# Early tiles of a routed expert layer taken from fewer blocks, with padded list rows and last-group scatters paced by other engines

## Chip, cores and metric

One core of one Trainium2 chip. The metric is the device time of one execution in microseconds (us), as the median of repeated runs; lower is better.

## What is computed

Two residual branches on x of shape (16, 128, 256), float32 throughout. The first is a long convolution over the products of eight context channels with each other, per head, contracted with the layer norm of x. The second, which the change touches, is a mixture of 32 experts (hidden 256, expert width 176) with six experts per token, chosen within four of eight groups, and a shared expert of double width:

```python
logits = xf @ w_router                       # xf: layer norm of x, 2048 tokens
scores = sigmoid(logits); sfc = scores + corr_bias
# four of eight groups by the sum of their two best, then the best six experts of these
combine[t, topk_idx] = scores[t, topk_idx]
eo = einsum('etm,emh->eth', silu(g) * u, down_w)        # g, u: xf by gate_w, up_w
routed = einsum('te,eth->th', combine, eo)
shared = silu(xf @ sh_gate_w) * (xf @ sh_up_w) @ sh_down_w
x = x + tanh(g_ffn) * (routed + shared)
```

## The kernel before

The 2048 tokens are 16 blocks of 128 (`B` = 16), handled in `NG` = 4 groups of `GB` = 4 blocks. The work has two parts.

**Groups.** `group(g, attend, route)` is written out on TensorE (PE), ScalarE (ACT) and VectorE. A call routes group g and does the attention of group g + 1; the last one, group 3, only routes. Routing a group means: normalize its rows into `payload` (even groups) or `payload_2` (odd groups), transpose them, logits (L1118), scores (L520), choice of six experts per token (`choose`), ranks of the tokens in their experts' lists by small matmuls (L1140 to L1147), slots (`place_rows`, L765), and the shared expert block by block (`shared_up`, `shared_hT`, `shared_down`, with `silu`, `copy_sh_hT` on ACT and `shared_times`, `add_shared` on VectorE). GpSimd (POOL) then scatters each block's rows, with token number and scores behind the 256 values, into the experts' lists in DRAM (`expert_lists`, L395): 24 scatters per group of 128 rows each, at most `AHEAD` = 6 in flight. When all of a group have landed it increments `payload_free` (L400), which so counts 1 before group 0 and g + 2 after group g.

**Tiles.** Afterwards each tile takes 128 rows of one expert's list: SP loads it (`load_tile`, L313) into one of `NX` = 4 slots of `payload`, PE transposes it (`xT`, L1196), VectorE copies it (L973), PE multiplies by gate and up weights (L1207), ACT and VectorE make silu(g) * u (L554, L991), PE transposes (L1217) and multiplies by the down weights (L1226), ACT scales by the token's score (L569), and POOL adds the rows into `token_sums` (L410). VectorE's `pick` reads score and token number from the loaded rows. Results wait in a ring of `YR` = 16 rows of buffers. SP loads a tile once tile t - 4 is transposed and picked.

The tile table is made on the chip. To start early, `NA` = 16 tiles come from full tiles among the lists of the groups known first: after group 2, i.e. from `KNOWN` = 12 blocks, with PE's counting matmuls at L1149 to L1154 and `describe_known` (from L827) and `spread_known` on VectorE, over the first `EA` = `WD_MID` = 18 experts. The rest is described by `describe_tiles` after the last group's ranks, `spread_tables` signals `tables_ready`.

**Weights.** All experts' weights end up in SBUF in one `arena`, on top of the buffers of the first part, so they can be loaded only as these come free. Gate and up weights of experts 0 to 13 (`EARLY` = 14) are loaded early. After the last attention, SP loads down weights of experts 0 to 17 and gate and up weights of 14 to 17 (L323, L324); ACT loads gate and up weights of 18 to 31 after the last group's scores (L524) and the remaining down weights in two DMAs (L545, L548) before its tile loop. PE waits for SP's loads before tile 0 (L1253, L1254) and for ACT's three before tile 16 (`last_in`, L1202).

SP's order around the change: down and up weights (L322 to L324), wait for the early table (L325), wait for `payload_free` of group 2 (L326), tiles 0 to 15, then wait for the whole table and for group 3's scatters (L333), tiles 16 on. POOL's order: scatters of groups 0 to 3, then the adds.

Of the kernel before, what the change touches and what calls it, by code (L numbers as in the profile page):

```python
# [9 lines left out]
GB = 4  # L10
# [17 lines left out]
ROW = L + 1 + E  # L28
TOK_AT, SCORE_AT = L, L + 1
# [30 lines left out]
assert ROUTER_AT + KC * E <= ARENA  # L60
# [3 lines left out]
WD_LAST = (X2T_AT - WD_AT) // WD_E // 2 * 2  # L64
assert WD_AT <= TMP_AT
# [13 lines left out]
assert TE_AT + NTILES <= WORK and NX <= GB  # L79

# [6 lines left out]
KNOWN = (NG - 1) * GB  # L87
EA = WD_MID
# [3 lines left out]
def build(nc, x, ctx_t, toeplitz, g_xattn, g_ffn, skip_d, w_router, corr_bias,  # L92
# [10 lines left out]
    with ctx:  # L103
# [18 lines left out]
        y_rows = sb("y_rows", [P, 3, L])  # L122
# [115 lines left out]
        y_at = [(y_rows, i * L) for i in range(3)] + [(blank, 0)]  # L238
        y_at += [(b, i * L) for b in (q_sb, shgu_sb, shd_sb) for i in range(4)]
        y_row = lambda t: win(*y_at[t % YR], [[1, L]])  # L240
        pick_w = lambda t: win(work, TW_AT + t % NPICK, [[1, 1]])
# [31 lines left out]
        def _(sp):  # L273
# [34 lines left out]
            def load_tile(t):  # L308
# [4 lines left out]
                sp.dma_start(payload[:, t % NX, :], lists[bass.ds(first, P), :]).then_inc(t_loaded[t % NX], 16)  # L313
# [9 lines left out]
            load_down(sp, 0, WD_MID, late_in)  # L323
            load_up(sp, EARLY, WD_MID, late_in)  # L324
            sp.wait_ge(tables_a_ready, 1)  # L325
            sp.wait_ge(payload_free, NG)  # L326
            for t in range(NX):
                load_tile(t)
            for t in range(NX, NA):
                load_tile(t)  # L330
# [21 lines left out]
        def _(pool):  # L352
# [25 lines left out]
            link(nc.gpsimd.tensor_scalar(tok_id[:, :], win(lane_dump, 0, [[0, B]]), float(B), None, ALU.mult))  # L378
            link(nc.gpsimd.tensor_tensor(tok_id[:, :], tok_id[:, :], iota_e[:, 0:B], ALU.add))
# [7 lines left out]
            for g in range(NG):  # L387
                pool.wait_ge(slots_ready, g + 1)
                pool.sem_inc(held, 1)
                for b in range(GB):  # L390
                    for k in range(TOPK):
                        sent = (g * GB + b) * TOPK + k
                        if sent >= AHEAD:
                            pool.wait_ge(scattered[sent % AHEAD], sent // AHEAD * 16)
                        nc.gpsimd.indirect_dma_start(  # L395
# [35 lines left out]
        def _(act):  # L431
# [18 lines left out]
            def group(g, attend, route):  # L450
# [51 lines left out]
                if route:  # L502
# [17 lines left out]
                    nc.scalar.activation(pay[g % 2][:, :, SCORE_AT:ROW], win(bank[4], 0, [[E, GB], [1, E]]),  # L520
                                         ACT.Sigmoid).then_inc(scores_ready, 1)
# [775 lines left out]
```

## Time and profile before

| | us |
|---|---|
| median of 3 runs (544.68 to 546.29) | 544.88 |
| profiled execution, its own time | 550.49 |
| profiled execution, span of the program | 548.6 |
| PE busy, TensorE's mean granted clock 0.903 | 445.5 (81%) |
| VectorE busy | 312.8 (57%) |
| POOL busy | 288.6 (53%) |
| ACT busy | 203.9 (37%) |
| DMA moved 85.38 MB | mean 156 GB/s |

Busy time counts instructions, not waits; matmuls are pipelined and their ends are modelled, so a busy PE isn't PE at its peak. Times within the execution are counted from the span's start. DMA share is the mean busy share of the core's 16 DMA engines. PEclk is the granted part of TensorE's full clock.

### The profile page before, as it was taken

How to read it: one execution, taken by the hardware profiler on the slowest of the kernel's cores; microseconds unless marked ns; L12 is line 12 of the kernel's file. 1: busy time of each engine (PE TensorE's matmuls, PEld its weight loads, DVE VectorE, ACT ScalarE, POOL GpSimd, SP SyncE). 2: the span in 40 equal slices, each digit the busy share in tenths (PEclk: the TensorE clock that was granted, in tenths of full speed). 3: DMA queues.
4: the chain of work that ended last, by engine and by line, in shares of the span. 5: the costliest groups of instructions: out<-in, count | busy, mean ns of one | idle time of the engine just before them, and what ended most of it. 6: DMA issues, size and time to landing. Idle time of an engine off the chain costs nothing.

```text
span 548.6 us, 8656 instructions
## 1 busy us (share of the span) xinstructions
PE 445.5 (81%) x2114; PEld 334.4 (61%) x2114; DVE 312.8 (57%) x1163; ACT 203.9 (37%) x522; POOL 288.6 (53%) x224
## 2 busy tenths in 40 slices
PE   0924989798888668646999999999999999999900
PEld 0724767666766456424777777777777777777700
DVE  3999999859968755303444444444444444444307
ACT  3531725533462322002444444444444444444400
POOL 2000038848884752771556566665656566656630
PEclk9985989989988959755999999999999999999965
DMA  7999302222221499983666666566656665666569
GB/s 260 357 302 404 156 32 84 97 87 101 90 98 55 146 257 340 357 292 106 108 116 107 118 110 121 108 118 106 121 108 118 107 121 106 119 108 122 67 145 351
DMA packets 56053, 85.38 MB, mean 156 GB/s; under 512 B 6492, under 2 KB 47676, under 8 KB 55740
## 3 DMA queue, kind: packets, MB, share of 16 engines
q1 hardware_dynamic: 33566, 46.68, 28.8%
q0 software_dynamic: 20160, 28.37, 26.7%
q10 hardware_dynamic: 2270, 9.68, 4.6%
q8 instruction: 23, 0.38, 0.3%
q14 instruction: 34, 0.28, 0.2%
HBM read 44.91 MB, written 39.80 MB: 154 GB/s over the span
## 4 chain that ended last, share of the span: by engine, by line
PE 61%; DVE 22%; issue 7%; DMA 4%; ACT 2%; another core or an unknown queue 2%; SPq 1%; POOL 1%; DVEq 0%; POOLq 0%; ACTq 0%
PE bank L1207 24%; PE bank L1226 17%; DVE arena L658 5%; PE bank L1196 5%; PE bank L1217 4%; PE bank L1069 3%; DVE arena L636 3%; PE bank L1090 3%; DVE arena L666 3%; DMA arena<-token_sums 2%; DVE arena L615 1%; DMA rows<-x 1%; PE bank L1079 1%; PE bank L1040 1%
## 5 line engine op out<-in xcount | busy, mean ns | idle before, releaser
L395 POOL DMA_INDIRECT expert_lists<-payload,slots x96 | 116.7, 1216 | 126.3 <-DVE slots L765 84.3
L1207 PE MATMUL bank<-wgu,work 128*128 x432 | 149.8, 470 | 6.8 <-issue 5.2
L1226 PE MATMUL bank<-wd,work 88*128 x432 | 111.9, 382 | 0.0
L991 DVE TENSOR_TENSOR work<-work,bank 128x176 f32<-128x176 f32 x108 | 36.4, 337 | 128.2 <-ACT work L554 113.6
L1207 PEld LDWEIGHTS bank<-wgu,work 128*128 128x128 f32 x432 | 75.2, 194 | 31.8 <-issue 9.5
L554 ACT ACTIVATE work<-bank 128x176 f32<-128x176 f32 x108 | 34.2, 317 | 125.5 <-PE bank L1207 96.9
L1226 PEld LDWEIGHTS bank<-wd,work 88*128 88x128 f32 x432 | 73.9, 191 | 6.2 <-issue 0.2
L973 DVE COPY work<-bank 128x256 f32<-128x256 f32 x108 | 45.8, 424 | 34.4 <-PE bank L1196 18.6
L410 POOL DMA_INDIRECT token_sums<-q_sb,dest x28 | 43.6, 1558 | 27.2 <-ACT q_sb L569 7.3
L410 POOL DMA_INDIRECT token_sums<-shgu_sb,dest x28 | 43.6, 1559 | 24.8 <-DMA token_sums<-shgu_sb,dest 6.8
L1217 PEld LDWEIGHTS bank<-ident,work 128*88 128x88 f32 x216 | 26.5, 123 | 37.7 <-issue 18.8
L410 POOL DMA_INDIRECT token_sums<-shd_sb,dest x24 | 37.4, 1558 | 22.2 <-DVE work L985 7.7
L410 POOL DMA_INDIRECT token_sums<-y_rows,dest x21 | 32.8, 1561 | 29.7 <-ACT y_rows L569 15.3
L1217 PE MATMUL bank<-ident,work 128*88 128x128 f32 x216 | 41.8, 275 | 6.6 <-DVE work L991 6.6
L1040 PE MATMUL bank<-arena 128*128 128x288 f32 x128 | 45.8, 442 | 1.5 <-DVE arena L643 1.0
L1069 PE MATMUL bank<-shgu_sb,arena 128*128 128x352 f32 x128 | 46.5, 512 | 0.0
L658 DVE TENSOR_TENSOR arena<-arena,q_sb 128x448 f32<-128x448 f32 (+7 forms) x120 | 45.4, 454 | 0.0
L1196 PE MATMUL bank<-ident,payload 128*128 128x128 f32 x216 | 42.8, 280 | 0.7 <-issue 0.7
L561 ACT COPY work<-bank 88x256 f32<-88x256 f32 x108 | 39.7, 367 | 0.1
L1196 PEld LDWEIGHTS bank<-ident,payload 128*128 128x128 f32 x216 | 31.3, 146 | 12.6 <-issue 2.1
L457 ACT COPY arena<-bank 128x288 f32<-128x288 f32 x64 | 25.3, 399 | 26.7 <-PE bank L1041 23.4
L1069 PEld LDWEIGHTS bank<-shgu_sb,arena 128*128 128x128 f32 x128 | 26.2, 216 | 12.5 <-issue 4.0
(170 smaller groups left out, 570.1 us busy)
## 6 DMA issues: line engine op xcount, KB each, us to landing
payload<-expert_lists SPq DMA_DIRECT2D x108, 144.5 KB
wgu<-w_gu SPq DMA_DIRECT2D x1, 4928.0 KB, 19.1
wgu<-w_gu ACTq DMA_DIRECT2D x1, 4928.0 KB
expert_lists<-blank SPq DMA_DIRECT2D x1, 4768.5 KB, 25.4
arena<-token_sums SPq DMA_DIRECT2D x8, 512.0 KB, 7.3
wd<-w_down SPq DMA_DIRECT2D x1, 3168.0 KB
token_sums<-blank SPq DMA_DIRECT2D x1, 2304.0 KB, 28.9
arena<-toeplitz ACTq DMA_DIRECT2D x2, 1024.0 KB, 10.5
```

The source lines that it names most:

```text
L395: nc.gpsimd.indirect_dma_start(lists, bass.IndirectOffsetOnAxis(ap=slots[:, g % 2, b, k:k + 1], axis=0), pay[g % 2][:, b, :], None).then_i ...
L410: nc.gpsimd.indirect_dma_start(sums, bass.IndirectOffsetOnAxis(ap=dest[:, t % NPICK:t % NPICK + 1], axis=0), y_row(t), None, compute_op=AL ...
L561: nc.scalar.copy(win(work, HT_AT + t % 2 * L, [[1, L]], parts=MH), bank[4 + t % 2][0:MH, 0:L]).then_inc(t_hT_copied, 1)
L658: last = nc.vector.tensor_tensor(win(arena, Z_AT + z0, [[DH * DH, CELLS], [1, DH - d]]), y, win(q_sb, q_at + i0, [[DH, CELLS], [1, DH - d] ...
L973: nc.vector.tensor_copy(win(work, XT_AT + t % 2 * L, [[1, L]]), bank[t % 2][:, 0:L]).then_inc(t_x, 1)
L991: nc.vector.tensor_tensor(win(work, H_AT + t % 2 * M, [[1, M]]), win(work, SG_AT + t % 2 * M, [[1, M]]), bank[2 + t % 2][:, M:2 * M], ALU. ...
L1040: nc.tensor.matmul(y[:, 0:2 * CB], toe(h, 0), prods(s, hh, 0, 2), start=True, stop=False)
L1069: last = nc.tensor.matmul(bank[5 + half][:, 0:SHM], x2T(b, k), shgu_sb[:, k, half * SHM:(half + 1) * SHM], start=(k == 0), stop=(k == KC - 1))
L1196: last = nc.tensor.transpose(bank[t % 2][:, k * P:(k + 1) * P], payload[:, t % NX, k * P:(k + 1) * P], ident[:, :])
L1207: last = nc.tensor.matmul(bank[2 + t % 2][:, 0:2 * M], xT_half(t, k), wgu[:, bass.ds(e * WGU_E + k * 2 * M, 2 * M)], start=(k == 0), stop= ...
L1217: last = nc.tensor.transpose(bank[4 + t % 2][0:MH, c * P:(c + 1) * P], win(work, H_AT + t % 2 * M + c * MH, [[1, MH]]), ident[:, :])
L1226: last = nc.tensor.matmul(bank[6 + t % 2][:, 0:L], hT_half(t, c), wd[:, bass.ds(e * WD_E + c * L, L)], start=(c == 0), stop=(c == 1))
```

## The change

Rows of the lists get 304 elements (1216 bytes) instead of 289 (1156); the added 15 are zeroed once. The early table is made after group 1, from 8 blocks and over 14 experts. Tiles 0 to 7 are loaded into four slots at the end of the arena instead of `payload`, once group 1's scatters have landed; tiles 8 to 15 go to `payload`, once group 2's have. SP loads only the down weights of experts 0 to 13; all others go in pairs of experts from ACT, six DMAs in the last group, the others one or two per tile in tiles 0 to 8. POOL's scatters of the last group, but the first, wait for VectorE's steps of the shared expert (`sh_h_ready`) and, from the 13th, for PE's tile transposes (`t_xT`). The ring of 16 result rows is laid out over other buffers, as `y_rows` has one less.

```diff
-ROW = L + 1 + E
-TOK_AT, SCORE_AT = L, L + 1
+ROW = -(-(L + 1 + E) // 16) * 16
+TOK_AT, SCORE_AT, SCORE_END = L, L + 1, L + 1 + E
...
+TILES_AT = ROUTER_AT + KC * E
+assert TILES_AT + 4 * ROW <= ARENA
...
+WD_TILES = (ROUTER_AT - WD_AT) // WD_E // 2 * 2
+LATE = [n for n in range(EARLY, E, 2)]
...
+IN_ARENA = 2 * NX
...
-KNOWN = (NG - 1) * GB
-EA = WD_MID
+KNOWN = (NG - 2) * GB
+EA = EARLY
...
+        tile_rows = lambda t, at, n: (win(arena, TILES_AT + t % NX * ROW + at, [[1, n]]) if t < IN_ARENA
+                                      else payload[:, t % NX, at:at + n])
...
             sp.wait_ge(pairs_summed, 2 * NG)
-            load_down(sp, 0, WD_MID, late_in)
-            load_up(sp, EARLY, WD_MID, late_in)
+            load_down(sp, 0, EARLY, late_in)
+            sp.wait_ge(payload_free, NG - 1)
             sp.wait_ge(tables_a_ready, 1)
+            for t in range(IN_ARENA):
+                load_tile(t)
             sp.wait_ge(payload_free, NG)
-            for t in range(NX):
-                load_tile(t)
-            for t in range(NX, NA):
+            for t in range(IN_ARENA, NA):
                 load_tile(t)
...
+            for p in pay:
+                nc.gpsimd.memset(p[:, :, SCORE_END:ROW], 0.0)
...
+                        nth_of = b * TOPK + k
+                        if g == NG - 1 and 0 < nth_of < GB * TOPK // 2:
+                            pool.wait_ge(sh_h_ready, g * GB + 1 + nth_of // 3)
+                        elif g == NG - 1 and nth_of:
+                            pool.wait_ge(t_xT, 1 + (nth_of - GB * TOPK // 2) // 2)
...
+                    if not attend:
+                        act.wait_ge(pairs_summed, 2 * NG)
+                        load_up(act, EARLY, EARLY + 2, last_in)
...
                     silu(0)
                     if not attend:
-                        load_up(act, WD_MID, E, last_in)
+                        load_up(act, EARLY + 2, EARLY + 4, last_in)
...
+                        if not attend:
+                            load_up(act, EARLY + 4 + 2 * b, EARLY + 6 + 2 * b, last_in)
...
+            def late_weights(t):
+
+                if t < 3:
+                    n = EARLY + 12 + 2 * t
+                    load_up(act, n, n + 2, last_in)
+                if t < len(LATE):
+                    n = LATE[t]
+                    if n == WD_LAST:
+                        act.wait_ge(sh_stored, 16 * (B - GB))
+                        act.wait_ge(sh_added, GB)
+                    if n == WD_TILES:
+                        act.wait_ge(t_xT, IN_ARENA)
+                        act.wait_ge(t_picked, IN_ARENA)
+                    load_down(act, n, n + 2, last_in)
+
             act.wait_ge(tables_ready, 1)
-            load_down(act, WD_MID, WD_LAST, last_in)
-            act.wait_ge(sh_stored, 16 * (B - GB))
-            act.wait_ge(sh_added, GB)
-            load_down(act, WD_LAST, E, last_in)
...
                     copy_y(t - 2)
+                if t < NA:
+                    late_weights(t)
...
-                    if g == NG - 2:
+                    if g == NG - 3:
                         nc.vector.tensor_copy(count_a[:, :], bank[4][:, 2 * GB * E:(2 * GB + 1) * E])
...
-                    pe.wait_ge(last_in, 48)
+                    pe.wait_ge(last_in, 2 * len(LATE) * 16)
...
-            pe.wait_ge(late_in, 32)
+            pe.wait_ge(late_in, 16)
```

## Rows read from the trace of the kernel before

**Rows 1.** Busy time by stretch; columns as in the first line.

```profile
core 0: us, PE busy (x) PEld busy (x) DVE busy (x) ACT busy (x) POOL busy (x), PEclk, DMA share, GB/s
...
100.00:150.00 50.00, 42.45 (x206) 33.17 (x204) 41.50 (x132) 21.46 (x47) 36.57 (x27) 0.93 0.25 90
190.00:200.00 10.00, 5.44 (x25) 4.64 (x24) 3.17 (x20) 4.25 (x8) 4.84 (x6) 0.50 0.94 254
...
207.00:226.00 19.00, 16.46 (x103) 12.63 (x103) 11.53 (x53) 3.13 (x6) 6.99 (x8) 1.00 1.02 374
...
230.00:240.00 10.00, 4.72 (x12) 2.22 (x10) 1.29 (x5) 0.00 (x0) 7.56 (x9) 0.50 0.82 301
...
230.47:257.19 26.72, 12.68 (x30) 6.81 (x28) 4.61 (x20) 1.57 (x5) 13.44 (x14) 0.50 0.66 230
...
250.00:260.00 10.00, 8.43 (x26) 5.75 (x27) 3.36 (x17) 2.31 (x7) 1.25 (x1) 0.61 0.23 65
...
300.00:400.00 100.00, 100.00 (x485) 74.07 (x483) 46.04 (x202) 42.69 (x121) 62.67 (x41) 1.00 0.65 114
```

**Rows 2.** Chain of waits late in the tile loop: start us, us, what.

```profile
509.44 1.19 PE bank L1207 x4
...
511.93 1.19 PE bank L1207 x4
```

**Rows 3.** Page, DMA queue of ACT (packets, MB, share) and DMA issues.

```profile
q10 hardware_dynamic: 2270, 9.68, 4.6%
...
payload<-expert_lists SPq DMA_DIRECT2D x108, 144.5 KB
...
wgu<-w_gu ACTq DMA_DIRECT2D x1, 4928.0 KB
expert_lists<-blank SPq DMA_DIRECT2D x1, 4768.5 KB, 25.4
```

**Rows 4.** Chain of waits from 190 to 260 us.

```profile
193.96 5.06 another core or an unknown queue
...
230.47 0.43 PE bank L1196 x2
...
240.49 9.01 issue
...
250.55 1.41 PE bank L1196 x2
...
257.40 0.43 PE bank L1196 x2
```

**Rows 5.** Timeline: start us, us, instruction, [idle before <- releaser]; scatters, loads, early table.

```profile
163.52 0.96 POOL L395 DMA_INDIRECT expert_lists<-payload,slots  x1 [0.30 <-issue]
...
188.38 0.32 SPq L260 DMA_DIRECT2D wd<-w_down  x1
...
205.95 0.39 ACTq L255 DMA_DIRECT2D wgu<-w_gu  x1
...
207.16 0.07 DVE L877 MEMSET tile_dump<- 128x16 f32 x1
...
217.84 43.18 SPq L313 DMA_DIRECT2D payload<-expert_lists  x9
...
217.96 0.96 POOL L395 DMA_INDIRECT expert_lists<-payload,slots  x1 [10.19 <-issue]
...
247.04 0.96 POOL L395 DMA_INDIRECT expert_lists<-payload,slots  x1 [0.30 <-issue]
```

**Rows 6.** Timeline: the early table's steps on VectorE, first steps of the tile loop.

```profile
188.44 0.38 DVE L847 TENSOR_TENSOR arena<-count_a,tile_at 128x216 f32<-128x216 f32 x1
...
198.16 0.19 DVE L860 TENSOR_TENSOR taken_a<-arena 128x32 f32<-128x32 f32 x1 [1.82 <-remote]
...
199.65 0.29 DVE L868 COPY arena<-arena 128x256 f32<-128x256 f32 x1
...
235.11 0.42 DVE L973 COPY work<-bank 128x256 f32<-128x256 f32 x1 [3.08 <-issue]
...
249.15 0.32 ACT L554 ACTIVATE work<-bank 128x176 f32<-128x176 f32 x1 [22.32 <-issue]
```

More of the change, by code:

```diff
@@ L59 @@
 ROUTER_AT = SHOUT_AT + 2 * L
-assert ROUTER_AT + KC * E <= ARENA
+TILES_AT = ROUTER_AT + KC * E
+assert TILES_AT + 4 * ROW <= ARENA
 STATS_AT, MOMENTS_AT, NEWTON_AT = TMP_AT, TMP_AT + 6 * B, TMP_AT + 8 * B
@@ L121, in build @@
         payload_2 = sb("payload_2", [P, GB, ROW])
-        y_rows = sb("y_rows", [P, 3, L])
+        y_rows = sb("y_rows", [P, 2, L])
         blank = sb("blank", [P, ROW])
@@ L237, in build @@
         hT_half = lambda t, c: win(work, HT_AT + t % 2 * L + c * P, [[1, P]], parts=MH)
-        y_at = [(y_rows, i * L) for i in range(3)] + [(blank, 0)]
-        y_at += [(b, i * L) for b in (q_sb, shgu_sb, shd_sb) for i in range(4)]
+        y_at = [(y_rows, i * L) for i in range(2)] + [(blank, 0)]
+        y_at += [(b, i * L) for b, n in ((q_sb, 4), (shgu_sb, 5), (shd_sb, 4)) for i in range(n)]
         y_row = lambda t: win(*y_at[t % YR], [[1, L]])
+        tile_rows = lambda t, at, n: (win(arena, TILES_AT + t % NX * ROW + at, [[1, n]]) if t < IN_ARENA
+                                      else payload[:, t % NX, at:at + n])
         pick_w = lambda t: win(work, TW_AT + t % NPICK, [[1, 1]])
@@ L312, in load_tile @@
                 first = table_value(sp, tile_row, t, E * LIST)
-                sp.dma_start(payload[:, t % NX, :], lists[bass.ds(first, P), :]).then_inc(t_loaded[t % NX], 16)
+                sp.dma_start(tile_rows(t, 0, ROW), lists[bass.ds(first, P), :]).then_inc(t_loaded[t % NX], 16)
             def load_block(n):
@@ L519, in group @@
                     act.wait_ge(logits_ready, g + 1)
-                    nc.scalar.activation(pay[g % 2][:, :, SCORE_AT:ROW], win(bank[4], 0, [[E, GB], [1, E]]),
+                    nc.scalar.activation(pay[g % 2][:, :, SCORE_AT:SCORE_END], win(bank[4], 0, [[E, GB], [1, E]]),
                                          ACT.Sigmoid).then_inc(scores_ready, 1)
@@ L708, in flat @@
                         return win(arena, o, [[step, n]])
-                    scores = pay[g % 2][:, :, SCORE_AT:ROW]
+                    scores = pay[g % 2][:, :, SCORE_AT:SCORE_END]
                     sfc = tmp(GB, E)
@@ L977, in pick @@
                 mask = win(work, MASK_AT + t % 2 * E, [[1, E]])
-                nc.vector.scalar_tensor_tensor(mask, iota_e[:, :], tile_e[:, t:t + 1], payload[:, t % NX, SCORE_AT:ROW],
+                nc.vector.scalar_tensor_tensor(mask, iota_e[:, :], tile_e[:, t:t + 1], tile_rows(t, SCORE_AT, E),
                                                ALU.is_equal, ALU.mult).then_inc(t_masked, 1)
@@ L981, in pick @@
                     dve.wait_ge(t_added[t % NX], nth(t - NPICK))
-                nc.vector.tensor_scalar(dest[:, t % NPICK:t % NPICK + 1], payload[:, t % NX, TOK_AT:TOK_AT + 1],
+                nc.vector.tensor_scalar(dest[:, t % NPICK:t % NPICK + 1], tile_rows(t, TOK_AT, 1),
                                         tile_dump[:, t:t + 1], float(t % S * SUM_ROWS), ALU.max, ALU.add)
@@ L1148, in group @@
                                             start=False, stop=True)
-                    if g == NG - 2:
+                    if g == NG - 3:
                         for seen in range(KNOWN):
@@ L1196, in xT @@
                     last = nc.tensor.transpose(bank[t % 2][:, k * P:(k + 1) * P],
-                                               payload[:, t % NX, k * P:(k + 1) * P], ident[:, :])
+                                               tile_rows(t, k * P, P), ident[:, :])
                 last.then_inc(t_xT, 1)
```

## The prediction

> **What bounds the kernel now.** I read the windows first. From 300 to 400 us TensorE is busy all the time at the full clock (2.4 GHz) with DMA at 0.65 [rows 1]; the matmuls of two tiles in a row start 2.49 us apart [rows 2], and the 108 tiles [rows 3] take half of the span. Nothing in the diff touches that stretch. The stretch between the shared experts and the running tile loop is different: from 230.47 to 257.19 us PE shows 12.68 us of work in 26.72, all at the low clock (1.2 GHz), with DMA at 0.66 and, from 230 to 240, at 0.82 [rows 1]. The chain puts the first tile's transposes at 230.47 and those of the fifth at 257.40, 26.9 us for four tiles that cost 4 x 2.49 = 10.0 us in the steady loop: **17.0 us are lost here**. The chain's largest piece is 9.01 us of "issue" at 240.49; tile 3 is reached at 250.55, so a tile took (250.55 - 230.47)/3 = 6.7 us [rows 4].
>
> Why is it slow? The queues [rows 5] show what flies. Group 1's last scatter leaves at 163.52. A pair of experts has 704 KB of gate and up weights (4928/7 [rows 3]) and, by the shapes, 352 KB of down weights. At 188.38 SP puts nine pairs down and behind them two pairs up on its queue, 4.6 MB; at 205.95 ACT adds seven pairs up, 4.9 MB. POOL waits 10.19 us for group 2's scatters to land, until 217.96, and only then does SP start the tile loads (217.84), although the table that they need is done at 207.16. The last group's 24 scatters go out back to back from 217.96 to 247.04. The engine rows [rows 6] show the second symptom, which I weigh most: signals come late. PE's transposes of tile 0 stand at 230.47, the copy that waits for them at 235.11; ACT's first silu stands at 249.15 after 22.32 us idle, for which the profile finds no releaser. The same is seen earlier: from 190 to 200 (DMA 0.94) ScalarE waits 5.06 us for logits and a VectorE step waits 1.82 us for VectorE's own signal [rows 4, 6]. But from 207 to 226, with DMA at 1.02, PE is busy 16.46 of 19 us at the full clock [rows 1]. So a full DMA alone doesn't make signals late; late stretches are those in which POOL's scatters run on and on beside weight loads. That is read from three stretches of one trace, not proved.
>
> **The change, part by part.**
> Early tiles from groups 0 and 1 and 14 experts: the tables come from 1024 tokens. The reference, run on the drawn inputs, sends 794, 836 and 722 of them to experts 0, 1 and 11: 6 + 6 + 5 full tiles, at least 16. So the 16 early tiles are all real, 91 remain, and the loop still runs 108. Cost of tiles: 0. The counting matmuls move from group 2 to group 1 and shrink from 12 to 8; the comparison at L847 (0.38 us [rows 6]) shrinks from 216 to 112 columns. Both under 0.3 us; 0.
>
> First eight tiles in the arena: their loads wait for group 1's scatters (over soon after 163.52) and the table, so they start at about 207.2 instead of 217.84 [rows 5]. Only four are in flight at a time, but these have 22 us until PE is free; before, they had 12 under the heaviest load. This covers the first wait.
>
> Weights in pairs from ACT: SP's load at 188 shrinks from 4.6 MB to 2.5 MB (down weights of 14 experts), ACT adds one pair (0.7 MB) before the logits. That lightens 188 to 200, where the planner's chain runs from 188.44 to 199.65 + 0.29 [rows 6], 11.5 us, and the shared experts cannot start before it. What can come back: at least 0, at most about the 5.06 us wait [rows 4]. I take 3.0, a little above the middle, as 2.1 of 4.6 MB go and 0.7 come. ACT issues 18 loads instead of three. One costs 0.39 us [rows 5]; two per tile in the first three tiles make 1.07 (42.69 us per 100 us, at 2.49 per tile [rows 1]) + 0.78 = 1.85 us of the 2.49: hidden. If the cover goes, it is 0.8 us for three tiles. Past 229 us there remain three pairs up and nine pairs down, 5.4 MB; ACT's queue moved 9.68 MB in 4.6% of 548.6 us, 25.2 us [rows 3], so they need 14.1 us of all engines. They are due at tile 16, 40 us later, and PE's one wait for all 18 stands there.
>
> The Trainium skill ("DMA: Bandwidth & Descriptors", section Bandwidth) speaks against the pairs: it wants at least 1 MiB per DMA for 75% of the peak, and these are 0.7 and 0.35 MB. At its 341 GB/s for 1 MB, as an estimate by that page, the 5.4 MB would take 15.9 us and not 14.1. By it the sum is the same, and the busy stretch ends some 2 us later, which makes the slower rival more likely.
>
> Scatters of the last group: each of the first 12 waits for a third of a shared block, each later pair for one more transposed tile. What is queued behind on POOL: the other scatters, and then all adds into token_sums. Who waits: SP's loads from tile 16 on, and ACT's ring of 16 result rows. The 24th scatter goes out with tile 5's transposes, some 13 us into the loop; landing took at most 10.19 [rows 5]; the first add so starts near tile 9, under the 16 rows of the ring, and POOL, busy 62.67 us in 100 [rows 1], catches up. Price: 0; if the first add slips 15 us further, PE waits for it.
>
> Rows of 1216 bytes: 5.2% more bytes in blanks, scatters and tile loads. The blanks landed in 25.4 us [rows 3], so 1.3 us later, long before the first scatter, under VectorE's work. In the loop DMA goes from 0.65 to at most 0.68: hidden. Whether aligned rows move faster no row shows: between 0 and the 5.2% they cost; I take 0. Two small memsets on POOL at the start: hidden by SP's earlier loads.
>
> **The sum**, in the profiled execution. Lost now: 17.0. After the change still lost: the first hand-overs, half of 235.11 - 230.47 [rows 4, 6] = 2.3, rounded to 2.5 with the load of the tile's number; the low clock at the start, as between 250 and 260, where a mean of 0.61 means 7.8 us at half clock [rows 1], so 3.9 us; and remaining lateness, between 0 and the 10.6 that are left of 17.0: I take a quarter, 2.6, as half of the scatters and a third of the bytes are gone by then. That is 9.0. Gain 17.0 - 9.0 + 3.0 = 11.0. The profiled execution took 550.49 us for a span of 548.6, 1% over the median of 544.88. 550.49 - 11.0 = 539.5, times 544.88/550.49 gives **534.0**. Within this case: 529 (no lateness, all of 5.06) to 540 (6 us of lateness, nothing at the front).
>
> **Rivals.**
> Everything prompt and the clock never falls: PE passes from the shared experts to tiles without a pause. Gain 17.0 - 2.5 + 3.0 = 17.5, 527.5. For: tiles are there. Against: before, PE's clock was low already at the first tile [rows 1], after the wait for VectorE's tables, and that wait stays. 0.13.
>
> Contention only moves. Tiles still take 6.7 us until the traffic ends. The work after 229: 14.1 us of weights, 12 scatters at 0.25 x 50/27 = 0.46 us each (100 to 150 us, 27 POOL instructions [rows 1]), 5.6 us, and eight tile loads at a third of 0.65 x 2.49 = 1.6 us per tile, 4 us: until 229 + 24 = 253. By then 3.6 tiles are done; before, the steady line stood at 4 - (257.4 - 253)/2.49 = 2.2. Gain 1.4 x 2.49 = 3.4: 541.5. For: the same bytes, fewer moved before 229. 0.20.
>
> **Slower.** The same rate, but it feeds itself: weights and scatters are now released by the tiles' own steps. At 6.7 us per tile the last scatter leaves at 229 + 5 x 6.7 = 262, the last weights later still, and the catching-up adds join. If the crawl ends at 265, 5.4 tiles are done where before had 4 + 7.6/2.49 = 7.1: 4.2 us lost, 549.0. It decides at 258.4, where both lines meet. For: all late rows lie where scatters and weights fly together, and the new order brings both into the loop. Against: slower release also thins the traffic. 0.15.
>
> The change doesn't reach the wait: tile loads were not what PE waited for, and lateness has another cause that stays. Then 544.9. For: the longest pieces carry no tile load as releaser. 0.05.
>
> The forecast has the remaining 0.47. A measurement of this kernel tells 0.3%, 1.6 us, from no change; faster by more: 0.47 + 0.13 + 0.20 less 0.04 of the moved contention = 0.76; within: 0.05 + 0.04 = 0.09; slower: 0.15. The range goes from 524.5, one below the best rival with all of the front's 5.06 (gain 19.6, 525.5), to 546.5, which leaves out most of the slower case.
>
> **What would show it.** Tile loads starting at about 207 and group 2's scatters landed before 210. The planner's chain under 9 us. From the first tile's transposes to the fifth's 14 to 20 us instead of 26.9. L554's idle time without one wait of 22 us. Last weights landed before tile 16. Still 108 tiles at 2.49 us. The forecast is wrong if a tile takes over 5 us in the first eight, if the gap at 230 remains with little DMA about (then lateness isn't contention), or if PE waits at tile 16 or for the ring.

## The result, and the profile after

The changed kernel took **552.46 us** (median of four runs, 550.64 to 557.7) beside 545.59 us for the kernel before: ratio **1.0111** [1.0058, 1.0164], slower by about 1.1%. The forecast was 534.0 us. The ratio is estimated from the single runs in the faster of the chip's two states and so is not the quotient of the two medians. The profiled execution of the changed kernel took 551.01 us for a span of 549.0. That of before had taken 550.49 us for 548.6, above its own median, so the two profiles are equally long while the medians are 1.1% apart. The profiles show how the work moved; for a difference of one per cent I go by the ratios of runs on one chip.

The page of the changed kernel, its span, queues, chain and DMA issues. ACT's late weights, before three loads of which one had 4928 KB [rows 3], are now eighteen small ones, and the blanks are 5% larger by the longer rows (4768.5 KB before), though they landed in 23.3 us and not 25.4 [rows 3]:

```profile
span 549.0 us, 8688 instructions
...
PEclk9985989899989668789999999999999999999755
DMA  7999212222223686598666666666667665675559
...
q10 hardware_dynamic: 2907, 11.84, 6.4%
...
PE 62%; DVE 18%; DMA 7%; issue 5%; ACT 3%; another core or an unknown queue 3%; POOL 1%; SPq 1%; DVEq 0%; POOLq 0%; ACTq 0%
...
wgu<-w_gu ACTq DMA_DIRECT2D x9, 704.0 KB
expert_lists<-blank SPq DMA_DIRECT2D x1, 5016.0 KB, 23.3
...
wd<-w_down ACTq DMA_DIRECT2D x9, 352.0 KB
```

Busy time by stretch, the changed kernel (columns as in the first line). These answer to [rows 1]:

```profile
core 0: us, PE busy (x) PEld busy (x) DVE busy (x) ACT busy (x) POOL busy (x), PEclk, DMA share, GB/s
...
230.00:240.00 10.00, 8.74 (x29) 5.57 (x28) 3.73 (x16) 0.90 (x3) 6.36 (x7) 0.63 0.64 208
240.00:250.00 10.00, 6.52 (x31) 4.47 (x30) 3.14 (x15) 3.06 (x9) 5.16 (x6) 1.00 1.02 342
250.00:260.00 10.00, 9.43 (x45) 6.45 (x44) 3.77 (x17) 3.66 (x11) 2.96 (x2) 1.00 0.81 273
300.00:400.00 100.00, 100.00 (x484) 74.08 (x483) 46.28 (x203) 42.57 (x121) 62.30 (x40) 1.00 0.66 117
```

From 230 to 260 TensorE does 24.7 us of work, where before it did 16.0, and from 240 on it is at the full clock (2.4 GHz), where before it was at the low one until 250 and for most of the time to 260. The gap at which the forecast aimed has mostly closed: the transposes of the first tile start at 230.40 and those of the fifth at 240.42, 10.0 us in place of 26.9. What is left of it comes after. The chain of waits has the third tile's transposes, a tile load and the ninth tile's transposes (start us, us, what):

```profile
235.43 0.43 PE bank L1227 x2
...
246.70 8.59 DMA payload<-expert_lists
...
255.34 0.44 PE bank L1227 x2
```

Six tiles took 19.9 us where the steady loop takes 14.9, and the ninth tile, the first that is loaded into `payload`, waited 8.59 us for its load, beside late weights and scatters (DMA at 1.02). The steady loop is unchanged. Yet the end did not move. The chain also shows what ends last in the changed kernel (start us, us, what; L598 writes the result row, L423 adds it into `token_sums`, L348 starts the reading of the sums):

```profile
507.34 0.88 PE bank L1257 x4
508.22 0.02 issue
508.24 0.48 ACT shgu_sb L598
508.72 0.60 issue
509.33 3.67 DMA token_sums<-q_sb,dest
...
513.85 1.46 POOL token_sums L423
...
520.72 3.70 DMA token_sums<-shgu_sb,dest
...
525.27 3.76 DMA token_sums<-shgu_sb,dest
...
529.22 0.34 SPq L348
...
532.82 10.27 DMA arena<-token_sums
```

PE's last matmul ends near 509.1; before it ended at 521.0. **TensorE is 11.9 us earlier** in this pair of profiles, and for 20 us nothing but adds runs: one every 2.3 us. An add holds POOL for 1.56 us and has landed about 3.7 us after its start, and the add after next waits for that landing, because the sums are kept in two copies (S = 2). The last add starts at 525.27; before, at 525.38. How the delay arose is in the timeline of POOL, changed kernel (start us, us, instruction, [idle before <- releaser]):

```profile
247.77 0.96 POOL L408 DMA_INDIRECT expert_lists<-payload,slots  x1 [0.30 <-issue]
256.74 1.61 POOL L423 DMA_INDIRECT token_sums<-y_rows,dest  x1 [8.01 <-issue]
258.66 1.58 POOL L423 DMA_INDIRECT token_sums<-y_rows,dest  x1 [0.30 <-issue]
265.59 1.56 POOL L423 DMA_INDIRECT token_sums<-blank,dest  x1 [5.35 <-DVE work L1016]
267.94 1.56 POOL L423 DMA_INDIRECT token_sums<-q_sb,dest  x1 [0.80 <-issue]
...
300.21 1.56 POOL L423 DMA_INDIRECT token_sums<-y_rows,dest  x1 [0.40 <-issue]
```

And the same of before:

```profile
258.75 1.61 POOL L410 DMA_INDIRECT token_sums<-y_rows,dest  x1 [10.75 <-ACT y_rows L569]
261.50 1.58 POOL L410 DMA_INDIRECT token_sums<-y_rows,dest  x1 [1.14 <-ACT y_rows L569]
263.98 1.56 POOL L410 DMA_INDIRECT token_sums<-y_rows,dest  x1 [0.89 <-ACT y_rows L569]
```

Before, the adds wait for result rows (the first was ready at 257.9). In the changed kernel the first row is ready at 243.9, but POOL still has scatters until 247.77 and then waits 8.01 us for them to land. The third add waits again, 5.35 us, for the landing of the first: the profile names a step of VectorE (L1016, the pick), but the pick of this add's own tile had ended at 239.0, and in a repeat, below, the profile names the landing itself. The seventeenth add, that of the first tile behind the 16 early ones, starts at 300.21, against 299.5 before. From there to the last add it is 225.1 us for 91 adds, 2.47 us each, while PE makes a tile in 2.49. From there on the adds run 13 to 16 us behind the results to the end, where before it was mostly 1 to 3 us: before, the adds kept up with the rows, now they wait for each other.

**Theory A**: the chain of adds sets the end. The changed kernel ends some 249 us after its seventeenth add starts, whatever PE does. The letters of the rivals are those of the recorded expectations. **B**: the loss is a disturbance that only unprofiled runs had. **C**: POOL's own pace or the DMA limits the adds, and not the wait for a landing. **D**: the pacing of the scatters is what helped PE, and without it PE is late again. **E**: the longer rows cost time. **F**: the late weights in small loads, beside the first adds, slow these down. Two more have no letter: PE's gain is lost elsewhere and the adds only follow, and POOL's wait for the landing of the scatters ahead of the first add is what delays the adds.

### The profile page after: what moved, and what is told of

Its sections match the earlier page's. It is cut to its first block, busy times and chain, and to the rows that moved or that the text cites. A ratio compares the mean times of both kernels' runs of the same rounds, so it can differ in the third digit from the quotient of the medians.

```text
span 549.0 us, 8688 instructions
## 1 busy us (share of the span) xinstructions
PE 442.6 (81%) x2110; PEld 333.2 (61%) x2110; DVE 312.2 (57%) x1163; ACT 203.8 (37%) x522; POOL 286.8 (52%) x226
## 3 DMA queue, kind: packets, MB, share of 16 engines
q10 hardware_dynamic: 2907, 11.84, 6.4%
## 4 chain that ended last, share of the span: by engine, by line
PE 62%; DVE 18%; DMA 7%; issue 5%; ACT 3%; another core or an unknown queue 3%; POOL 1%; SPq 1%; DVEq 0%; POOLq 0%; ACTq 0%
PE bank L1238 23%; PE bank L1257 16%; PE bank L1121 4%; PE bank L1100 4%; PE bank L1227 4%; PE bank L1248 4%; DVE arena L689 4%; DVE arena L667 2%; PE bank L1071 2%; DVE arena L697 2%; DMA arena<-token_sums 2%; PE bank L1110 2%; DMA payload<-expert_lists 2%; PE bank L1091 1%
## 5 line engine op out<-in xcount | busy, mean ns | idle before, releaser
L408 POOL DMA_INDIRECT expert_lists<-payload,slots x96 | 114.7, 1195 | 128.9 <-DVE slots L796 88.9
L1238 PE MATMUL bank<-wgu,work 128*128 x432 | 147.8, 465 | 1.3 <-DVE work L1004 1.3
L423 POOL DMA_INDIRECT token_sums<-shgu_sb,dest x35 | 54.5, 1558 | 34.4 <-ACT shd_sb L598 10.8
L423 POOL DMA_INDIRECT token_sums<-q_sb,dest x28 | 43.6, 1558 | 24.6 <-DMA token_sums<-q_sb,dest 8.5
L423 POOL DMA_INDIRECT token_sums<-shd_sb,dest x24 | 37.4, 1557 | 21.0 <-DVE work L1016 6.4
L1227 PE MATMUL bank<-ident,payload 128*128 128x128 f32 x200 | 38.5, 273 | 0.2 <-DMA payload<-expert_lists 0.2
L470 ACT COPY arena<-bank 128x288 f32<-128x288 f32 x64 | 25.4, 399 | 25.9 <-PE bank L1072 22.3
L1227 PEld LDWEIGHTS bank<-ident,payload 128*128 128x128 f32 x200 | 28.3, 142 | 10.9 <-DMA payload<-expert_lists 1.0
L1121 PE MATMUL bank<-shd_sb,arena 88*128 88x256 f32 x128 | 32.2, 396 | 1.9 <-issue 0.7
## 6 DMA issues: line engine op xcount, KB each, us to landing
expert_lists<-blank SPq DMA_DIRECT2D x1, 5016.0 KB, 23.3
```

The costliest lines, as they stand in the source:

```text
L408: nc.gpsimd.indirect_dma_start(lists, bass.IndirectOffsetOnAxis(ap=slots[:, g % 2, b, k:k + 1], axis=0), pay[g % 2][:, b, :], None).then_i ...
L423: nc.gpsimd.indirect_dma_start(sums, bass.IndirectOffsetOnAxis(ap=dest[:, t % NPICK:t % NPICK + 1], axis=0), y_row(t), None, compute_op=AL ...
L1121: last = nc.tensor.matmul(bank[4][:, 0:L], win(arena, HST_AT + c * P, [[1, P]], parts=MH), shd_sb[0:MH, c, :], start=(c == 0), stop=(c == 3))
L1227: last = nc.tensor.transpose(bank[t % 2][:, k * P:(k + 1) * P], tile_rows(t, k * P, P), ident[:, :])
L1238: last = nc.tensor.matmul(bank[2 + t % 2][:, 0:2 * M], xT_half(t, k), wgu[:, bass.ds(e * WGU_E + k * 2 * M, 2 * M)], start=(k == 0), stop= ...
```

## Experiments

Ratios are to the kernel before on the same chip, with their 95% interval. Chips differ (the kernel before had medians from 537.22 to 551.05 us on them), so profiles are compared within one chip where a few us decide.

**The changed kernel again.** No edit.

> The changed kernel once more, as the base of the others on the same chip. Theory A (the chain of adds sets the end): each add into token_sums waits for the landing of the one two before it, which makes about 2.48 us per add, as much as PE needs per tile; PE ends near 508 us, the last add goes out near 525, and the profiled span stays near 549. Theory B (the loss is a disturbance that only unprofiled runs had): the ratio to before comes out near 1.00 here. A alone gives a ratio of 0.995 to 1.005; the first result was 1.011, and a ratio above 1.006 says that something more than A costs time.

Measured: 1.0107 [1.0051, 1.0163], 554.79 us beside 549.82. The seventeenth add started at 301.4, and PE ended at 510.6 of a span of 551.9. The slowdown is real and of the size first seen, and B falls. The expectation had set 0.995 to 1.005 for A alone and read anything above 1.006 as a second cause. So A explains why PE's gain doesn't reach the end, and not yet why the kernel got slower; the second cause is F, measured further down.

**Three copies of the sums.** An add waits for the third before it; reading takes a copy more.

```diff
-S = 2
+S = 3
...
+                nc.vector.tensor_tensor(a, a, d, ALU.add).then_inc(f_added, 1)
+                dve.wait_ge(f_added, 2 * c + 2)
```

> The changed kernel with three copies of token_sums (S = 3), so that an add waits for the one three before it. Theory A: adds go at 1.9 us until they have caught up with PE, the last add goes out within 3 us of PE's end (near 511), 14 us earlier than with two copies; the third copy adds 2 MB to be read at the end and one more addition per part, 5 to 8 us. Sum 6 to 9 us faster than the changed kernel, about 0.985 to 0.99 of it. Theory C (POOL's own pace or DMA throughput limits the adds, not the wait): adds stay at 2.4 us or more, and the kernel gets 5 to 8 us slower.

Measured: 0.9973 [0.9942, 1.0004]; changed kernel on that chip 1.0107, so 0.987 of it, as expected under A. The timeline of POOL with three copies, near the end:

```profile
509.89 1.56 POOL L423 DMA_INDIRECT token_sums<-shgu_sb,dest  x1 [0.94 <-ACT shgu_sb L598]
512.15 1.56 POOL L423 DMA_INDIRECT token_sums<-shgu_sb,dest  x1 [0.70 <-issue]
514.02 1.56 POOL L423 DMA_INDIRECT token_sums<-shgu_sb,dest  x1 [0.30 <-issue]
515.88 1.56 POOL L423 DMA_INDIRECT token_sums<-shgu_sb,dest  x1 [0.30 <-issue]
```

The last add starts 12.3 us earlier than in the repeat of the changed kernel (528.2), and the seventeenth came 1.3 us after its row. But reading three copies takes 25.5 us from its start at 520.0 to the end, where two take 19.8, and PE ends 2.3 us later. Where the adds are behind, they start 1.86 us apart (the last three lines), with the same 1.56 us on POOL: it is the wait for a landing that made 2.47, and C falls. So the adds were the bound, and the third copy gives part back at the end.

**No pacing.** The waits ahead of the last group's scatters go.

```diff
-                        nth_of = b * TOPK + k
-                        if g == NG - 1 and 0 < nth_of < GB * TOPK // 2:
-                            pool.wait_ge(sh_h_ready, g * GB + 1 + nth_of // 3)
-                        elif g == NG - 1 and nth_of:
-                            pool.wait_ge(t_xT, 1 + (nth_of - GB * TOPK // 2) // 2)
```

> The changed kernel without the waits of the last group's scatters on sh_h_ready and t_xT. Theory A: the first add starts as much earlier as the last scatter lands earlier. Without the waits 24 scatters from 209.5 at 1.26 us end at 240, against 244 to 248 with them, so the adds start at 244 to 250 instead of 256.7, and the end comes 5 to 10 us earlier, if signals are not late. Theory D (the pacing keeps signals prompt): PE's first four tiles go back to 6.7 us each and PE ends near 518; then the adds end no earlier than with the waits, within 2 us.

Measured: 1.0277 [1.0209, 1.0345], far slower. If nothing but the last scatter held the adds back, this had to be faster, since it leaves at 241.58. But the first add starts at 265.84 and the last at 542.31. The windows without pacing (columns as before):

```profile
230.00:240.00 10.00, 0.00 (x0) 0.00 (x0) 0.00 (x0) 0.00 (x0) 7.63 (x8) 0.50 0.53 190
240.00:250.00 10.00, 1.08 (x4) 0.62 (x4) 1.82 (x6) 0.58 (x1) 1.93 (x3) 0.50 0.13 47
```

and its timeline (PE's transposes of the tables, and VectorE's step that reads them):

```profile
224.76 0.83 PE L1199 MATMUL bank<-ident,arena 128*128 128x128 f32 x6
246.38 0.29 DVE L974 CAST tile_row<-bank 128x128 int32<-128x128 f32 x1 [22.30 <-remote]
```

For ten microseconds PE, VectorE and ScalarE do nothing while POOL scatters. PE's transposes of the tables are done at 225.6, but the step of VectorE that reads them starts at 246.38, after 22.30 us idle; PE then waits for VectorE, and ScalarE for PE. Everything goes on 4 us after the last scatter. DMA is at 0.53, and of weights only one load of 704 KB flies there. The first gate-and-up matmul starts at 255.9 (changed kernel: 232.7). D holds, and more strongly than it was put: PE ends at 531.4, expected near 518, and the last add starts 14 us later than in the repeat of the changed kernel, expected within 2 us.

**Plain writes instead of adds.**

```diff
-                    y_row(t), None, compute_op=ALU.add)
+                    y_row(t), None)
```

> The changed kernel with the rows written plainly into token_sums instead of added to it (the accumulation is left out, all waits stay). Theory A: a write without reading lands sooner (the list scatters move the same kind of rows), so the chain of two in flight runs at 2.0 us or less, catches up with PE, and the last one goes out near 511: 12 to 15 us faster. Theory C (POOL's pace is the limit, 1.56 us busy and what lies between): the adds stay at 2.4 us and nothing changes by more than 2 us.

This kernel leaves the accumulation out, so it is for the time alone. Measured: 0.9826 [0.975, 0.9902]. POOL needs 0.96 us in place of 1.56. The writes gain on the results: the seventeenth (297.2) is still 6.2 us behind its row, from the thirtieth on they are 0.8 us behind, and the last starts at 517.3, though the first started at 261.0, later than in the changed kernel. With a quicker chain a front that is no better gives a faster kernel. If PE's gain were lost elsewhere and the adds only followed, neither this nor the third copy could bring it back.

**Before, with the pacing alone.** The five lines above added to the kernel before.

> The kernel before with only the pacing of the last group's scatters added. Theory D (an unbroken run of POOL scatters holds back other engines' signals; pacing is what speeds the start of the tiles): the wait of ScalarE's first silu (22.3 us before) falls under 12 us, PE ends 5 to 12 us earlier than 521, near 511 to 516. With theory A on top, the adds still follow at 2.48 us from a start near 256 to 260, so the total stays within 1% of before. If D is wrong and the lateness comes from the bulk weight loads, PE ends at 520 or later and the first tiles still take over 6 us each.

Measured: 0.9999 [0.9965, 1.0033]. PE ends at 509.5, a little sooner than expected and near the changed kernel's 509.1 and 510.6 in its repeat; ScalarE's longest wait for the first silu is 9.8 us, expected under 12. The last scatter leaves at 250.8, the first add starts at 255.4, the seventeenth at 296.0, the last at 522.8. So the pacing alone makes all of PE's gain, and the time stays as it was: the adds run 9 to 11 us behind the results, where before it was 1 to 3. PE's gain buys nothing while the seventeenth add starts no earlier (295.4 on the same chip without pacing, next run).

**Before, with rows of 1216 bytes alone.**

```diff
-ROW = L + 1 + E
+ROW = -(-(L + 1 + E) // 16) * 16
...
```

> The kernel before with rows of 1216 bytes (and the ring laid out as after). Theory A has nothing for it: list scatters and tile loads carry 5% more, the adds 1024 bytes as before, so a ratio of 0.997 to 1.003. Rival E (padded rows cost in the loaded stretch, where scatters land late): 2 to 5 us slower, ratio 1.004 to 1.01, with group 2's scatters landed after 218.

Measured: 0.9968 [0.9933, 1.0003]. No loss, and E falls; a gain of 0.3% is neither shown nor excluded. This profile (546.34 us) is also the best stand-in for the kernel before at its usual time: first add at 253.2, seventeenth at 295.4, 2.1 us behind its row, PE's end at 516.2, span 544.5. Beside it the adds of the changed kernel on the same chip start 6 us later (301.4), and PE's gain is 5.6 us and not 11.9.

**The early table from three groups.** The changed kernel, with the first tile loads again behind group 2's scatters.

```diff
-KNOWN = (NG - 2) * GB
+KNOWN = (NG - 1) * GB
...
-            sp.wait_ge(payload_free, NG - 1)
+            sp.wait_ge(payload_free, NG)
...
```

> The changed kernel with the early table made from three groups again and the first tile loads behind group 2's scatters. They start then near 209 instead of 205, still 20 us before PE needs them: no difference, within 0.3% of the changed kernel (ratio to before about 1.01). If the earlier table matters, PE's first tile moves and the kernel gets 2 us or more slower than the changed one.

Measured: 1.0091 [1.005, 1.0131], as the changed kernel. Tile loads start at 211.6 in place of 205.7; the seventeenth add at 302.1; PE ends at 510.9. So making the early table a group sooner, the headline of the change, does nothing to the time.

**Late weights spread out.** One late load per tile.

```diff
-                if t < len(LATE):
-                    n = LATE[t]
+                elif t < 3 + len(LATE):
+                    n = LATE[t - 3]
```

> The changed kernel with one late weight DMA per tile (12 tiles) instead of two in each of the first three. Theory A with its start: from 240 to 250 DMA is at 1.02, the last scatter (247.8) lands only at 256.7 and the first two adds at 265; with the weights spread the adds' third starts at 262 to 264 instead of 265.6 and the end comes 1.5 to 4 us earlier than the changed kernel. If the weights don't delay them, no change; if tile 16 then waits for weights, PE's end moves but the adds' does not.

Measured: 1.0117 [1.0055, 1.0179], a miss: 1.5 to 4 us less were expected. Weights now go out until 266.3 (260.6 in the changed kernel), so they lie beside the adds for longer, and the seventeenth starts at 303.8.

**Late weights in bulk.** One load of 6336 KB of gate and up weights in the shared stage, and three of down weights, two of them ahead of the tile loop.

```diff
-                if t < 3:
-                    n = EARLY + 12 + 2 * t
-                    load_up(act, n, n + 2, last_in)
...
+                if t == 7:
...
+                    load_down(act, WD_TILES, E, last_in)
...
+            load_down(act, EARLY, WD_LAST, last_in)
```

> The changed kernel with the weights in bulk again (gate and up of 14 to 31 after the last scores, down in three DMAs). In all seven kernels with two copies so far the span is the start of the 17th add plus 249 to 251 us, so only that start counts. Theory F (late weights beside the first adds slow these down: the third add comes 9 us after the first, and not 5 as in the paced kernel before): with the weights landed before 250 the 17th add starts at 296 to 298 instead of 300 to 304, span 545 to 548, ratio 0.995 to 1.003. If F is wrong, it stays at 300 or later and the ratio at 1.01.

Measured, on a faster chip (before 537.22 us): 0.9971 [0.9944, 0.9999], as F had it. The seventeenth add starts at 285.5 of a span of 534.9; the expectation of 296 to 298 was for a slower chip. The changed kernel itself was not run on this one, so it is repeated side by side below.

**Adds first.** POOL's wait for the landing of the last scatters moves behind the first four adds, in the changed kernel.

```diff
             for t in range(4 * (SURE + 1)):
+                if t == 4:
+                    for landed in scattered:
+                        pool.wait_ge(landed, NG * (GB * TOPK // AHEAD * 16))
+                    pool.sem_inc(payload_free, 1)
                 add_tile(t)
```

> The changed kernel with POOL's wait for the last scatters' landing moved behind the first four adds. Theory A: the first add starts right after the last scatter's issue, near 249, instead of 256.7, unless the results are later; the 17th add comes 4 to 8 us earlier and the kernel gets 4 to 8 us faster than the changed one, ratio 0.996 to 1.003. If the pace of adds under the late weights is the limit and not their start, the gain is under 2 us.

Measured: 0.9964 [0.9929, 0.9999], as expected; seventeenth add at 284.7, span 533.9.

**Before, with pacing and adds first.**

> The kernel before, paced (as x5), with the first four adds ahead of the landing wait. Theory A: the adds start near 251 instead of 255.4, the 17th at 290 to 293 (x5: 296.0); with PE's end near 509.5 the last add goes out near 517. Span 540 to 543, ratio 0.985 to 0.993. If the adds of the first tiles run at 2.5 us whatever their start, and the start is bound by the results, no gain over x5.

Measured: 0.9913 [0.9885, 0.9941], as expected; seventeenth add at 281.4, end of the span at 529.6.

**Bulk weights and adds first together**, in the changed kernel.

> x9 and x10 together: the changed kernel with bulk weights and the first four adds ahead of the landing wait. Theory A with F: both gains add, 17th add at 290 to 294, span 539 to 543, ratio 0.983 to 0.993. Without F it equals x10.

Measured: **0.9899** [0.9855, 0.9943], 531.15 us beside 537.22, the best of all. Its timeline of POOL:

```profile
234.87 0.96 POOL L408 DMA_INDIRECT expert_lists<-payload,slots  x1 [0.30 <-issue]
236.14 1.62 POOL L424 DMA_INDIRECT token_sums<-y_rows,dest  x1 [0.30 <-issue]
238.06 1.58 POOL L424 DMA_INDIRECT token_sums<-y_rows,dest  x1 [0.30 <-issue]
241.10 1.56 POOL L424 DMA_INDIRECT token_sums<-blank,dest  x1 [1.46 <-DMA token_sums<-y_rows,dest]
```

The 8.01 us ahead of the first add are 0.30, the 5.35 ahead of the third 1.46 (on this faster chip). The seventeenth add starts at 279.7, and the span ends at 528.2, 248.5 us later.

**Small and bulk weights on one chip.** The changed kernel and the one with bulk weights, side by side.

> The changed kernel beside x14. Theory F: 17th add at 299 or later counted on a chip where before takes 549, ratio to before 1.006 to 1.014, and at least 1% above x14. If the two agree within 0.5%, F falls and the difference seen so far was the chip.

> x9 again beside x13. Theory F: ratio to before 0.994 to 1.000, its 17th add 3 us or more ahead of that of x13, in the profile of the same chip. If F is wrong, it is as slow as x13.

Measured: 1.007 [1.0037, 1.0103] and 0.9985 [0.9955, 1.0016]. The windows with small loads:

```profile
240.00:250.00 10.00, 7.97 (x36) 5.01 (x36) 3.60 (x18) 3.03 (x9) 5.90 (x7) 1.00 1.02 331
250.00:260.00 10.00, 7.88 (x39) 5.48 (x38) 3.43 (x15) 2.93 (x10) 1.93 (x3) 1.00 0.82 282
```

with bulk loads:

```profile
240.00:250.00 10.00, 6.55 (x22) 3.85 (x21) 2.29 (x10) 2.12 (x7) 5.06 (x6) 0.84 0.72 256
250.00:260.00 10.00, 10.00 (x50) 7.43 (x49) 4.58 (x20) 4.21 (x12) 5.15 (x4) 0.99 0.47 100
```

and POOL's timeline, small loads first:

```profile
257.88 1.61 POOL L423 DMA_INDIRECT token_sums<-y_rows,dest  x1 [7.76 <-ACT q_sb L598]
259.80 1.58 POOL L423 DMA_INDIRECT token_sums<-y_rows,dest  x1 [0.31 <-issue]
266.63 1.56 POOL L423 DMA_INDIRECT token_sums<-blank,dest  x1 [5.25 <-DMA token_sums<-y_rows,dest]
```

then bulk:

```profile
253.94 1.61 POOL L423 DMA_INDIRECT token_sums<-y_rows,dest  x1 [3.44 <-DVE work L1007]
255.86 1.58 POOL L423 DMA_INDIRECT token_sums<-y_rows,dest  x1 [0.30 <-issue]
258.54 1.56 POOL L423 DMA_INDIRECT token_sums<-blank,dest  x1 [1.10 <-DMA token_sums<-y_rows,dest]
```

While the first adds fly, DMA is at 0.82 with small loads and 0.47 with bulk. POOL's wait ahead of the first add is 7.76 against 3.44 us, ahead of the third 5.25 against 1.10. The seventeenth add starts at 302.3 against 296.3, the ends are 551.7 and 547.0. F holds in kind; the difference of 0.85% is a little under the "at least 1%" that it had. With bulk weights the changed kernel is as fast as the one before (0.9985), which is what A alone gives. So the late weights as small loads are the second cause: they make the slowdown.

**Two scatters in flight.** No pacing, but a scatter of the last group waits until the second before it has landed.

```diff
+                        if g == NG - 1 and b * TOPK + k >= 2:
+                            pool.wait_ge(scattered[(sent - 2) % AHEAD], ((sent - 2) // AHEAD + 1) * 16)
```

> The changed kernel without pacing, the last group's scatters limited to two in flight instead of six. If signals are late because of scatters piled up in the DMA queues, no wait of VectorE or ScalarE on PE over 10 us is left between 205 and 262 (x3: 22.3), and PE's first gate-up matmul starts within 4 us of that of x13 (x3: 23 us later than the changed kernel). If it is POOL's unbroken run as such that delays them, it is at least 10 us later than in x13.

Measured: 1.032 [1.0256, 1.0385]. The waits from 205 to 285 (engine, line, what it waited for: us in total, times, longest):

```profile
POOL expert_lists L405 <- DMA expert_lists<-payload,slots: 34.0, 14, 4.1
ACT work L580 <- PE bank L1235: 22.1, 11, 8.5
```

The 22 us standstill is gone: the first gate-and-up matmul starts at 233.0 (233.9 in the changed kernel on that chip), PE ends at 516.1. So the scatters as such don't make the standstill; in these runs it comes only with one unbroken run of them. Whether it is the number in flight, POOL's run without a pause or the rate is not separated, as all three change here. But the scatters run until 275.1, so the adds start at 279.6, the seventeenth at 319.9, and the end comes 247.9 us after it, at 567.8. A's sum holds at this far end too.

**Three copies on the best.** S = 3 in the kernel with bulk weights and adds first.

> x12 with three copies of token_sums. Theory A: x12's last add goes out 11 us behind PE's end; with three copies it follows within 3 us, 8 us earlier, and the third copy costs 6 us at the end (x2: 25.5 us from the start of reading to the end against 19.8). Net 0 to 4 us faster than x12, ratio to before 0.983 to 0.990.

Measured: 0.9923 [0.9889, 0.9957], on another chip than the 0.9899 with two copies, and a miss: 0.983 to 0.990 was expected. The last add does follow PE's end within 3.0 us (515.0), but the longer reading takes that back. A third copy brings nothing to be seen here.

**The theories.** Start of the seventeenth add and end of the span, in the kernels with two copies that add: before 299.5 and 548.6; changed 300.2, 549.0; pacing alone 296.0, 545.8; 1216 bytes 295.4, 544.5; three groups 302.1, 551.2; spread 303.8, 554.8; no pacing 315.4, 565.6; two in flight 319.9, 567.8; best 279.7, 528.2. The difference lies between 247.9 and 251.0 in all of them and in the six others of this kind, while the end of PE's work lies from 28 to 52 us ahead of the end. Where the adds follow the rows at once, as in the kernel before, PE's 2.49 us per tile would give the same distance; where they are behind, the constant is the adds' own. That this chain then is the bound is shown by the third copy and by the plain writes, which shorten it and bring the end forward.

## Why the prediction was wrong

**The gap in front of the tiles: right in kind, lucky in the number.** PE's loss was put at 17.0 us with 9.0 left after the change, so 8.0 gained, and 3.0 more at the front. In the pair of profiles PE's work ended 11.9 us earlier, which is near the 11.0 of the sum only because two errors cancel: 5.1 us were left and not 9.0, and the front gave nothing. From the first tile's transposes to the fifth's it took 10.0 us, better than the forecast's 14 to 20; the low clock ended at 240 instead of beyond 250. The cause was named only in part: "late stretches are those in which POOL's scatters run on and on beside weight loads", but hardly any weight loads are needed: without pacing the longest standstill came with DMA at 0.53 and one load in flight. That is the forecast's own sign that "lateness isn't contention", at least not for the DMA engines. The run with pacing alone shows that this one part of the change makes the gain.

**Adds behind the scatters: the step that failed.** The text was: "the first add so starts near tile 9, under the 16 rows of the ring, and POOL, busy 62.67 us in 100 [rows 1], catches up. Price: 0". The first add even started earlier, with five rows done, and PE never waited for the ring. But POOL does not catch up. Its busy share counts 1.56 us per add, and the adds are a chain: each waits for the landing of the second before it, and 91 of them took 2.47 us each, as long as a tile. The 12.8 us by which the first add trailed its row (243.9 to 256.7) are still there at the end (509.7 to 525.27 is 15.6). The slack of [rows 1], 37% of POOL, did not exist: it was waiting. The chain [rows 2] put PE on the critical path before; the adds ran 1 to 3 us behind it with no slack of their own.

That made the likeliest sum 11 us too low. Put right, PE's gain ends at a queue whose first add starts 2 us earlier than before (256.7 against 258.8), is held up once more, and whose seventeenth starts no earlier (300.2 against 299.5): 0 in the profiles. That is a forecast of no change, and with bulk weights no change is what was measured (0.9985). The slower rival named the wrong place: the tiles did not crawl; "the catching-up adds join" was in it, but not as the thing that decides.

**Weights in pairs: costed for bytes, not for what lies beside them.** They were put under PE's time. They fly beside the last scatters and the first adds, and there they cost 6 us of the adds' start (302.3 against 296.3). That is the rest of the miss, and what made the kernel slower and not merely no faster. The Trainium skill ("DMA: Bandwidth & Descriptors", section Bandwidth) asks for at least 1 MiB per DMA for 75% of the peak; by it, smaller loads should cost more of the engines' time per byte. The trace agrees: ACT's queue moved 11.84 MB in both kernels, in 6.5% of 551.7 us with pairs and 6.0% of 547.0 with bulk, 35.9 against 32.8 us.

**The front, 3.0 us: wrong.** The shared chain stands where it stood. ScalarE's wait for the logits grew instead, from 5.06 [rows 4] to 9.01 us; the chain of the changed kernel has

```profile
189.66 9.01 another core or an unknown queue
```

There, 1.4 MB less on the queues (2.1 MB gone, 0.7 come) took nothing off it. The planner's chain took 10.9 us (184.14 to 195.07), forecast under 9.

**The rest.** 16 real early tiles and 108 tiles at 2.49 us held. Tile loads started at 205.7, forecast 207.2, and by the run with three groups that is worth nothing. Rows of 1216 bytes at 0 held within 0.3%. Of the signs listed, PE waiting for the ring was near: the right sign to look for was the distance from a result row to its add.

**Open.** Why signals are late while scatters pile up: the runs show that it goes with an unbroken run of them, at a DMA share of only 0.53, and no more. Why the kernel before took 1% more in its profiled execution than in the others is not settled either. It may be the chip, whose number is not on record for that profile. In the other runs the profiled execution lies within 1% of its kernel's median. The profiles alone would call the two kernels equal. Which share of the 6 us is the size of the loads and which their place was not tried.

## What to carry to other kernels

An engine's busy share says nothing about slack if its instructions wait for one another's landings: take the time from one start to the next in steady state, compare it with the bound's, and if they are equal a late start is paid in full at the end. When work is taken off the critical path, ask which chain is next, and when that chain can start. In this kernel a long run of indirect scatters was best fed between other engines' steps, and what must follow them should not wait for their landing unless it reads it.

## What the runs showed of the hardware

During an unbroken run of indirect scatters, one every 1.26 us, with DMA at 0.53 in its middle, VectorE's step began 20.8 us after PE's matmuls before it had ended (22.3 us idle); with two scatters in flight the longest wait among PE, ScalarE and VectorE was 8.7 us. An accumulating indirect DMA of 128 rows held POOL for 1.56 us, a plain one for 0.96. The accumulating one had landed 3.7 us after its start in the tail; with DMA at 0.82 the third add, waiting for the first, started 8.8 us after it. Eighteen weight loads of 704 and 352 KB made their queue take 9% more of the DMA engines' time than the same bytes in four loads (35.9 against 32.8 us for the whole queue, 11.84 MB). The same kernel took between 537.22 and 551.05 us (medians) on different chips.
